# Feed-forward loads spread over the cross-attention groups, weights and masks in later chunks, constants by transfer, layer norm one chunk ahead

## What is computed

```
x = x + attn(layernorm(x))           # causal; scores = (g*q W_cross k + (1-g)*q M k) / 4, softmax
x = x + xattn(layernorm(x), ctx)     # 77 context tokens a batch; score = -1e9 where the mask is set
x = x + ffn(layernorm(x))            # down(silu(gate(x)) * up(x)), int weights / 127, hidden 768
```

## Time and profile before

| what | value |
|---|---|
| three runs | 1141.55, 1145.98, 1146.23 us; median 1145.98 |
| profiled execution | 1145.35 us, its span 1143.6 us |
| mean granted TensorE clock | 0.962 of 2.4 GHz |
| PE, DVE, ACT, POOL busy | 1044.8, 750.0, 573.4, 230.8 us |
| projection, self attention | 0 to about 121 us, then to about 646 us |
| middle, cross attention, feed-forward | to about 724, to about 900, to 1143.6 us |

### The profile page before, as it was taken

The page is one execution under the profiler, slowest core; times in us unless marked ns, Lnnn a source line. Parts: engine busy times, 40 slices in busy tenths (PEclk is TensorE's granted clock), DMA queues, the critical chain, the costliest instruction groups (busy, mean ns, idle before and its releaser), DMA issues. The chain is left out here.

```text
span 1143.6 us, 19037 instructions
## 1 busy us (share of the span) xinstructions
PE 1044.8 (91%) x7092; PEld 602.9 (53%) x7092; DVE 750.0 (66%) x1603; ACT 573.4 (50%) x1043; POOL 230.8 (20%) x192
## 2 busy tenths in 40 slices
PE   2889789999999999999999878898599899999997
PEld 2777234444444444444444455444243588888886
DVE  5997877777888878877785266555254355555552
ACT  1454146667767767667676549356256311111110
POOL 6654630000000000000000057200100133333331
PEclk9999679999999999999999998899699899999999
DMA  7279833433334444444110166666653201111101
GB/s 242 103 228 262 225 59 70 75 76 71 75 61 87 89 85 87 89 88 85 40 62 23 59 192 185 145 140 144 150 134 99 99 18 47 47 57 56 56 20 37
DMA packets 89636, 113.48 MB, mean 99 GB/s; under 512 B 13819, under 2 KB 74747, under 8 KB 88008
## 3 DMA queue, kind: packets, MB, share of 16 engines
q1 hardware_dynamic: 85896, 107.25, 37.6%
q10 hardware_dynamic: 3648, 5.02, 2.2%
HBM read 66.26 MB, written 45.45 MB: 98 GB/s over the span
## 5 line engine op out<-in xcount | busy, mean ns | idle before, releaser
L774 ACT ACTIVATE prob<-bank 128x512 f32<-128x512 f32 (+1 forms) x608 | 329.3, 575 | 184.8 <-PE bank L818 106.0
L726 DVE TENSOR_REDUCE pm<-bank 128x1 f32<-128x512 f32 (+3 forms) x608 | 364.6, 656 | 83.8 <-PE bank L802 63.7
L797 PE MATMUL bank<-stk,stq 96*128 96x512 bf16 (+3 forms) x768 | 227.3, 340 | 8.4 <-DVE pm L726 4.1
L814 PE MATMUL bank<-stq,stk 98*128 98x512 bf16 (+3 forms) x768 | 222.9, 329 | 0.9 <-ACT prob L774 0.8
L828 PE MATMUL bank<-prob,va 128*17 128x512 f32 (+3 forms) x1536 | 164.5, 501 | 0.0
L797 PEld LDWEIGHTS bank<-stk,stq 96*128 96x128 bf16 x768 | 70.2, 99 | 160.3 <-DVE pm L726 115.6
L1550 ACT ACTIVATE e_sg<-bank 128x512 f32<-128x512 f32 x48 | 28.7, 598 | 188.4 <-PE bank L132 188.4
L1308 ACT ACTIVATE xprob<-bank 80x512 f32<-80x512 f32 x128 | 73.8, 593 | 87.1 <-PE bank L1345 83.8
L957 POOL TENSOR_TENSOR c_rstd<-c_ve,mhalf 128x4 f32<-128x4 f32 x8 | 8.1, 1008 | 508.0 <-DVE c_ve L125 508.0
L814 PEld LDWEIGHTS bank<-stq,stk 98*128 98x128 bf16 x768 | 69.4, 98 | 56.9 <-issue 12.4
L1270 DVE TENSOR_REDUCE xpm<-bank 128x4 f32<-128x320 f32 x128 | 60.5, 489 | 53.8 <-PE bank L1331 52.1
(11 more groups left out here) (173 smaller groups left out, 1388.6 us busy)
## 6 DMA issues: line engine op xcount, KB each, us to landing
qk<-a_parts SPq DMA_DIRECT2D x32, 384.0 KB, 4.1
od<-u_out SPq DMA_DIRECT2D x16, 512.0 KB, 3.2
oin<-od SPq DMA_DIRECT2D x32, 256.0 KB
od<-xu SPq DMA_DIRECT2D x16, 512.0 KB, 2.7
xq<-c_parts SPq DMA_DIRECT2D x16, 384.0 KB, 3.1
xstq<-xq SPq DMA_DIRECT2D x32, 192.0 KB, 3.9
stq<-qk SPq DMA_DIRECT2D x28, 192.0 KB, 4.9
stk<-qk SPq DMA_DIRECT2D x14, 384.0 KB, 7.3
```

The costliest lines, as they stand in the source:

```text
L726: nc.vector.tensor_reduce(pm[:, k, h0:h0 + hb, r], src[:, 0:hb * w].rearrange("p (h w) -> p h w", h=hb), AX, ALU.max).then_inc(s_mxe, 1)
L774: nc.scalar.activation(prob[:, U % NPS, 0:hb * n], bank[STB[U % NSB]][:, 0:hb * n], ACT.Exp).then_inc(s_ex, 1)
L797: mm = nc.tensor.matmul(dst[:, h * w:(h + 1) * w], stq[i][0:R, half, h0 + h, r * P:(r + 1) * P], stk[i][0:R, h0 + h, k0:k0 + w], start=(h ...
L814: mm = nc.tensor.matmul(dst[:, h * n:(h + 1) * n], stk[i][0:RM, h0 + h, kt * P:(kt + 1) * P], stq[i][0:RM, half, h0 + h, q0:q0 + n], start ...
```

## The change

Six edits, in the order of the program:

- `normalise1` of chunk c + 2 stands at the end of chunk c (before the value additions) and no longer chunk c + 1 at its start.
- PE's two waits at the end of the projection (all splits, all value additions) become one (first split of the last chunk); the two stand again after the first maxima of group 0.
- The constants: `cross_constants` goes. POOL writes two small tiles (`ones`, `minus`) in the self-attention stage, and SP copies them from there into the constant rows of `mk` and `xstk` inside `load_later`, between the mask and the int weights. `mk` and `negid` have 96 partitions and no longer 128; `xstk` loses its spare head, so that the last score unit has 80 columns of weights.
- ACT and POOL prepare the feed-forward weights in chunks 3 to 5 (before 1 to 3), ACT the masks in chunk 2 (before 4); the third weight is loaded in chunk 4 (before 2).
- `plan2`: the transposition left over from the last group stands after score unit 2 (before 0), and the 9 ring items in units 2 to 7 (before 0 to 7).
- `load_ffn` of chunks 0 and 1: one pair of transfers (`oin2`, `din2`, 256 KB each) at the end of each of groups 7 to 10; before, all four pairs at the end of group 6.

```diff
@@ qkv_vector
+            normalise1(1)
             for c in range(NCH):
-                if c + 1 < NCH:
-                    normalise1(c + 1)
                 split(c, 0)
                 split(c, 1)
...
                 split(c, 3)
+                if c + 2 < NCH:
+                    normalise1(c + 2)
                 need(v, vo[c % 2], 16 * (c // 2))
@@ qkv_tensor
             t.wait_ge(s_xt, KT * NCH)
-            t.wait_ge(s_r, 4 * NCH)
-            t.wait_ge(s_ve, 2 * NCH)
+            t.wait_ge(s_r, 4 * (NCH - 1) + 1)
@@ self_gpsimd
             self_constants(g, 2, GB)
+            nc.gpsimd.memset(ones[:], 1.0).then_inc(s_pad, 1)
+            g.wait_ge(s_pad, 1)
+            nc.gpsimd.memset(minus[:], -1.0).then_inc(s_pad, 1)
+            g.wait_ge(s_pad, 2)
@@ self_tensor
+            t.wait_ge(s_r, 4 * NCH)
+            t.wait_ge(s_ve, 2 * NCH)
             t.wait_ge(s_set, GB)
@@ mid_sync
-                if c == 2:
+                if c == 4:
                     load_last_weight(sp)
@@ mid_gpsimd
-                if c == 0:
-                    cross_constants(g)
-                if 1 <= c < 4:
-                    ffn_weight_low(g, c - 1)
+                if 3 <= c < 6:
+                    ffn_weight_low(g, c - 3)
@@ mid_scalar
-                if 1 <= c < 4:
-                    ffn_weight_high(a, c - 1)
-                if c == 4:
+                if c == 2:
                     masks(a)
+                if 3 <= c < 6:
+                    ffn_weight_high(a, c - 3)
@@ plan2
-        NMX2, NST2, NPS2, LAG2, AHEAD = len(ring2), 2 * HG, 8, 3, 2
+        NMX2, NST2, NPS2, LAG2, AHEAD, LATE2 = len(ring2), 2 * HG, 8, 3, 2, 2
...
-            if u == 0:
+            if u == LATE2:
                 plan2.append(("r", NMX2 - 1, AHEAD - 1))
...
-            upto = (u + 1) * (NMX2 - 1) // NST2
+            upto = max(0, u + 1 - LATE2) * (NMX2 - 1) // (NST2 - LATE2)
@@ load_later
             sp.dma_start(mku[0:S2], mask_t).then_inc(s_mu, 16)
+            sp.wait_ge(s_pad, 2)
+            sp.dma_start(mk[S2:MR].rearrange("p b s -> p (b s)").rearrange("p (n s) -> p n s", s=512),
+                         ones[S2:MR, None, :].to_broadcast([MR - S2, B * S // 512, 512])).then_inc(xs_set, 16)
+            sp.dma_start(xstk[R:RM].rearrange("p h b s -> p (h b s)").rearrange("p (n s) -> p n s", s=512),
+                         minus[:, None, :].to_broadcast([2, H * B * SK // 512, 512])).then_inc(xs_set, 16)
@@ cross_sync
                     store_inverse(sp, b)
-                    if b == 0:
-                        load_ffn(sp, 0)
-                        load_ffn(sp, 1)
+                if 7 <= g < 7 + 2 * KT:
+                    load_ffn(sp, (g - 7) // KT, [(g - 7) % KT])
```

More of the change, by code:

```diff
@@ L46, in program @@
     RM = R + 2
+    MR = 96
     VW = 2 * HD
@@ L98, in program @@
         tri_k = sb(root, "tri_k", [P, HG, P], BF16)
-        negid = sb(root, "negid", [P, HG, SK], BF16)
+        negid = sb(root, "negid", [MR, HG, SK], BF16)
         sel = sb(root, "sel", [3 * H, KT, P], BF16)
         mhalf = sb(root, "mhalf", [P, J])
+        ones = sb(root, "ones", [P, 512], BF16)
+        minus = sb(root, "minus", [2, 512], BF16)
         xres = sb(root, "xres", [P, NCH, J, D])
@@ L314, in qkv_gpsimd @@
                 nc.gpsimd.tensor_copy(tri_k[:, h, :], trif[:, 1, :]).then_inc(s_con, 1)
-                nc.gpsimd.tensor_scalar(negid[:, h, :], ident[:, 0:SK], NEG, None, ALU.mult).then_inc(s_con, 1)
+                nc.gpsimd.tensor_scalar(negid[:, h, :], ident[0:MR, 0:SK], NEG, None, ALU.mult).then_inc(s_con, 1)
             nc.gpsimd.tensor_copy(identb[:], ident[:]).then_inc(s_con, 1)
@@ L641, in program @@
         s_set = sem("b_set")
+        s_pad = sem("b_pad")
         s_mxf = sem("b_mxf")
@@ L1193, in ffn_weight_low @@
                                     ALU.subtract).then_inc(s_fl, 1)
[L1195 to L1201, removed]
         def masks(a):
             a.wait_ge(s_mu, 16)
-            a.wait_ge(xs_set, 3)
             nc.scalar.activation(mk[0:S2], mku[0:S2], ACT.Identity).then_inc(s_mk, 1)
@@ L1342, in scores @@
                 at = (i * HG + h) * B * SK + b * SK
-                nc.tensor.matmul(dst[:], xstk[:].rearrange("p h b s -> p (h b s)")[0:RM, at:at + P],
+                cols = min(P, H * B * SK - at)
+                nc.tensor.matmul(dst[0:cols, :], xstk[:].rearrange("p h b s -> p (h b s)")[0:RM, at:at + cols],
                                  xstq[i][0:RM, half, h], start=True, stop=False, skip_group_check=True)
-                nc.tensor.matmul(dst[:], negid[:].rearrange("k h l -> k (h l)")[:, 0:P], mk[:, b, q],
+                nc.tensor.matmul(dst[0:cols, :], negid[:].rearrange("k h l -> k (h l)")[:, 0:cols], mk[:, b, q],
                                  start=False, stop=True, skip_group_check=True).then_inc(xs_st, 1)
@@ L1359, in cross_tensor @@
                 t.wait_ge(s_mk, 1)
-                t.wait_ge(xs_set, 3)
+                t.wait_ge(xs_set, 32)
                 for n in range(AHEAD * NMX2 - 1):
@@ L1414, in store_inverse, with load_ffn @@
             sp.dma_start(rdn2[b * H:(b + 1) * H].rearrange("h (c t) -> (h c) t", t=DT), den2[:, b]).then_inc(s_inv, 16)
-        def load_ffn(sp, c):
+        def load_ffn(sp, c, ks=range(KT)):
             b, u = c // 2, c % 2
@@ L1419, in load_ffn @@
             need(sp, es_op, 2 * (c - 1))
-            for k in range(KT):
+            for k in ks:
                 sp.dma_start(oin2[:, u, k], od2[b * GB + 2 * k:b * GB + 2 * k + 2, :, 0, :, u * CH:(u + 1) * CH]
@@ L1683, in program @@
         xmrow = sb(cross, "xmrow", [2 * HG * 4, 2, 2, P], BF16)
-        xstk = sb(cross, "xstk", [P, H + 1, B, SK], BF16)
-        mk = sb(cross, "mk", [P, B, S], BF16)
+        xstk = sb(cross, "xstk", [P, H, B, SK], BF16)
+        mk = sb(cross, "mk", [MR, B, S], BF16)
         xstq = [sb(cross, f"xstq{i}", [P, 2, HG, 512], BF16) for i in range(GB - 1)]
```

## The result

The changed kernel takes 1137.99 us (median of 20 runs, 1130.67 to 1147.33) against 1145.03 (20 runs, 1141.05 to 1148.57): ratio 0.9938, interval 0.992 to 0.9956. That is 7 us where 23 were forecast, and above the range of 1113 to 1130. The profiled execution took 1134.03 us, its span 1132.3.

What follows compares the result with a forecast made beforehand. PE, busy 1044.8 of 1143.6 us, was taken as the bound, its gaps and lower clock winnable. 1145.35 - 17.6 + 1.5 + 1 - 10.1 + 5.4 - 3.4 = 1122.2 us; own range 1118 to 1126, wider 1113 to 1130.

Steps and rivals of the forecast that it cites:

- plan2: Cross attention: three score units cover the transposition's fourteen waits for maxima; -10.1 us, bounds -11 and -5.
- Spreading the loads: Cross attention: one load pair a group removes the query-load stall, -17.6; pairs' transfers +1.5, POOL's multiplications +1.
- A query load has its issue time plus more than one group to land, so I expect little: +1.5: Cross attention, groups 7 to 10: query loads have slack against the added pairs; +1.5 us, bounds 0 and 8.
- rival B: Cross attention: pairs collide with query loads, a third to half of the stall returns; 1128 to 1131, chance 0.2.
- The +1 for POOL's multiplications: Cross attention: POOL's two multiplications beside DVE's casts of xmt can hold a cast; +1 us, bounds 0 and 4.7.
- The middle stage: Constants on one DMA engine delay oin of chunk 6 to 692.5, first cross product 729.2 instead of 723.89; +5.4 us.
- rival A: Middle stage: constants don't delay the queue (spread or passed by), giving -1.7; total 1115, chance 0.15.
- The start of self attention: The cast at 127.94, 3.55 us, ends before POOL's memset starts; -3.4 us, 0 if not, held 7 in 10.
- Layer norm a chunk ahead: Projection: removes PE's 1.1 us wait a chunk, but DVE decides; 0 us, bounds -4 and +1.
- Its work in a chunk is the same, turned round: Projection: DVE's work per chunk is unchanged by the new order, so the layer norm term is 0.
- POOL's quotients: Cross attention: POOL's two multiplications beside DVE's casts of xmt, costed at +1 us, bounds 0 and 4.7.
- the old stall: Cross attention near group 10: 13.1 us query-load wait plus products at half clock behind eight transfers; 17.6 us excess.

Runs made afterwards that it cites:

- b1: The kernel before with the new plan2 alone (LATE2 = 2): 1132.17 us, ratio 0.9889.
- e1: The changed kernel with the constants made by POOL memsets again, without the ones and minus transfers: 1129.95 us, ratio 0.9876.
- e7: The changed kernel with constants by memsets and the feed-forward load pairs in groups 7, 9, 11 and 13: 1120.52 us, ratio 0.9788.
- e4: The changed kernel with the eight feed-forward loads in one block at the end of group 6 again: 1146.78 us, ratio 1.0015.
- e11: The changed kernel with POOL's low parts of queries and keys left out (third parts zero): 1135.70 us, ratio 0.9913.
- e5: The changed kernel with the layer norm in its old place, at the start of the chunk before: 1134.75 us, ratio 0.9896.
- e10: The changed kernel with memsets, pairs in groups 7, 9, 11 and 13, old layer norm place, int weights behind oin: 1120.04 us, ratio 0.9792.
- b2: The kernel before with the feed-forward loads of two a group alone, pairs in a row: 1133.13 us, ratio 0.989.
- e8: The changed kernel with memsets, pairs in groups 7, 9, 11 and 13, int weights issued in chunk 1 behind oin: 1120.85 us, ratio 0.9785.

## Why the prediction was wrong

The direction was right, and the size was less than a third. Term by term:

- *`plan2`*, -10.1: the mechanism held, and the term was too small (b1: -12.4, outside the bounds of -11 and -5).
- *Spreading the loads*, -17.6 + 1.5 + 1: the stall went, but the step "A query load has its issue time plus more than one group to land, so I expect little: +1.5" failed. The slack was counted for one load; four pairs in a row leave no time between them to work off what each adds. Measured: -11.4 alone, -8.8 against the block in the changed kernel, and 9.4 more when a free group stands between pairs (e1 to e7), which makes -18.2 and meets the term without contention. So contention costs about 9 where 1.5 stood. Its upper bound was 8, and rival B, 6 to 9 us at a chance of 0.2, was the case that came. The +1 for POOL's multiplications is in these 9: in the changed kernel one of them holds one cast for 1.53 us and PE waits 1.26, which is the term and its size.
- *The middle stage*, +5.4 (its own figures give 729.2 - 723.89 = 5.3): the mechanism was right, constants on one engine ahead of `oin`, and it measured +11.3. Two parts were too small. DVE went on at 692.78, where 692.5 less the 2.4 of the earlier start was forecast, 2.7 later. From there to the first cross product 40.1 us passed for 36.7, and the clock was at half where PE had idled; in e1, with less of that, it took 38.4, so about half of this part was under-counted work. By e1, the constants cost 8.0 us by the medians and 9.8 in the stage, against 7.1 between forecast and rival A; without them the stage is 1.5 longer than before, not 1.7 shorter.
- *The start of self attention*, -3.4: the cast is 0.17 us. Right, by 0.3 us of room, and in two other profiled executions (e4 and e11) the memset caught it. With the layer norm in its old order the stage ends 4.5 us sooner than before (641.1 for 645.7).
- *Layer norm a chunk ahead*, 0: failed, the step "Its work in a chunk is the same, turned round". The work was the same and its neighbour on POOL was not: `a_xn` takes 1.3 us more, a chunk 0.9 more, which makes 3.2 us by the medians (e5) and 3.8 at the end of self attention, outside the bounds of -4 and +1.
- *The rest of the span*, +2.7: not forecast, and not the change's as far as is known. There is a stretch at a clock of 0.56 at 1115 to 1120 in the feed-forward, but its code is unchanged, and the kernel before with `plan2` alone (b1) has 1.6 more there as well.

Put together: contention 9.4 for 2.5 (it and POOL's quotients), constants and the middle 5.9 more, layer norm 3.2 more, the rest 2.7: 18.7 over, less 2.3 for `plan2`, makes 16.4; the shortfall is 16. Terms measured in different kernels carry 2 to 3 us each, and the last one is a single draw, so the closeness of that sum is partly luck.

Two of the misses, contention and the middle stage, share a step: a wait that the change would bring was priced at its length. (For the old stall the prediction did count products at half clock.) After the waits in the windows above, products ran at a clock near 0.5. Between e1 and e7 PE's waits in cross attention for `xstq`, `xmrow` and `xmt` differ by 2.6 us (5.8 and 3.2) and the kernels by 9.4; the changed kernel's median clock is 0.0085 below that of before and of e7. So it is shown that pairs in a row cost more than PE's added waits are long. That the waits bring the low clock, and not something else that the two have in common, is only argued, in cross attention as in the middle stage, and two kernels speak against a strict rule. e10, with pairs apart and waits of 1.1 and 1.2 us, still had a clock of 0.51 from 830 to 850. b2, with pairs in a row and 3.1 us of waits for `xstq`, had 1.00 from 780 to 880.

## What to carry to other kernels

Ask of each transfer what stands behind it in its queue, and of its partition count whether it can spread: 152 KB on 19 partitions, with 20 KB behind them, cost 8 us in front of a waited-for load, and two chunks later 1 us, which is within the scatter. When loads are spread over loop passes, leave a pass free between them if a pass has no spare bandwidth: it was worth 9.4 us here. The mean share of a stage does not show a backlog. Before a wait is called the one to remove, find it in the timeline: the list of waits gives the longest of a line, and in the expectation of e8 that was another chunk's. Before swapping two instructions of DVE, look which POOL instruction runs beside each.

## What was not expected of the hardware

- One kernel spread over 17 us (1130.67 to 1147.33) with a mean clock from 0.963 to 0.946, while the kernel before spread over 7.5.
- SP was held 5.96 us by the issue of a 20 KB transfer behind a transfer on 19 partitions, and 0.68 us behind the same bytes cut into 16 and 3.
- Behind the 19 partitions the DMA share was 0.06 to 0.07 for two microseconds: one engine of 16 at 22 GB/s.
- DVE's layer norm of a chunk took 1.37 us with POOL nearly idle, 1.76 and 3.05 beside different POOL work, and DVE's value additions took 2.0 either way.
